# An attention and expert-routing kernel: one exponential a unit, the diagonal of the maxima on GpSimd, and transposes moved behind the scores

## The reference

```
x = layernorm(x + attention(x, x, x, causal))                  # self
x = layernorm(x + attention(x, encoder_output, encoder_output)) # cross
x = layernorm(x + moe(x))                                      # 8 experts, 2 a token, FF = 512
attention: scores = q k / sqrt(8); a = softmax(scores); o = a v; o @ wo + bo
```

## Time and profile before

| what | value |
|---|---|
| time, median of 3 runs | 798.61 us (795.01 to 799.62) |
| the profiled execution | 803.89 us |
| its span | 802.1 us |
| TensorE busy (matmuls) | 596.7 us, 74% |
| weight loads | 471.7 us, 59% |
| VectorE | 488.9 us, 61% |
| ScalarE | 453.3 us, 57% |
| GpSimd | 370.1 us, 46% |
| mean granted clock of TensorE | 0.876 of full speed |

### The profile page before, as it was taken

How to read it: one execution, slowest core, us unless ns; L and a number is a source line. 1 busy time by engine, 2 the same in 40 slices (tenths; PEclk the granted TensorE clock), 3 DMA queues, 4 the chain that set the end, 5 groups by cost and what they waited for, 6 DMA issues and landing times. The chain is left out here.

```text
span 802.1 us, 21265 instructions
## 1 busy us (share of the span) xinstructions
PE 596.7 (74%) x7870; PEld 471.7 (59%) x7870; DVE 488.9 (61%) x1337; ACT 453.3 (57%) x824; POOL 370.1 (46%) x576
## 2 busy tenths in 40 slices
PE   2776676776767698887987988698777776878970
PEld 1344444545444476765766776476666666777870
DVE  3465879767696877888776578866334651221153
ACT  1223545444333589977997889688467554334320
POOL 7122243433337544435753665387237476530350
PEclk9965878877757999998999999899989888899995
DMA  4351554843132645544655675546546457778730
GB/s 111 106 174 54 161 170 128 287 125 87 34 93 66 198 146 168 164 130 139 195 155 177 185 205 171 151 140 174 162 142 191 141 176 222 234 239 266 234 96 20
DMA packets 141413, 124.64 MB, mean 155 GB/s; under 512 B 12224, under 2 KB 123600, under 8 KB 141312
## 3 DMA queue, kind: packets, MB, share of 16 engines
q1 hardware_dynamic: 134496, 113.06, 46.6%
q0 software_dynamic: 4368, 9.05, 4.1%
q10 hardware_dynamic: 2448, 1.18, 0.5%
HBM read 86.81 MB, written 38.54 MB: 156 GB/s over the span
## 5 line engine op out<-in xcount | busy, mean ns | idle before, releaser
L1089 DVE TENSOR_REDUCE row_max<-bank 128x16 bf16<-128x1024 f32 x64 | 78.3, 1224 | 79.4 <-PE bank L1501 78.6
L776 POOL TENSOR_TENSOR prob_lo<-probT,prob_hi 128x384 f16<-128x384 f32 x64 | 68.7, 1073 | 92.8 <-ACT prob_hi L892 92.4
L1549 PE MATMUL bank<-consts,o_n 128*128 128x64 f32 x256 | 47.7, 316 | 81.2 <-DVE o_n L1108 71.6
L1628 PE MATMUL bank<-w_in,w_hl 128*128 128x128 f32 x704 | 106.3, 298 | 0.0
L1549 PEld LDWEIGHTS bank<-consts,o_n 128*128 128x128 f32 x256 | 39.3, 220 | 95.3 <-issue 71.0
L1628 PEld LDWEIGHTS bank<-w_in,w_hl 128*128 128x128 f32 x704 | 93.8, 207 | 0.4
L889 ACT ACTIVATE probT<-bank 128x1024 f32<-128x1024 f32 x64 | 65.6, 1024 | 46.2 <-PE bank L1525 45.8
L762 POOL TENSOR_TENSOR veps<-mv,eps 128x1 f32<-128x1 f32 x64 | 14.5, 226 | 140.3 <-DVE mv L1127 140.3
L799 POOL DMA_INDIRECT w_hl<-ys,pos x60 | 59.6, 994 | 40.5 <-DMA ys<-w_hl 23.5
L1614 PE MATMUL bank<-xT,w_in 128*128 128x128 f16 x1056 | 77.9, 226 | 0.0
L1082 DVE TENSOR_TENSOR prob_lo<-probT,prob_hi 128x640 f16<-128x640 f32 x64 | 62.3, 973 | 24.9 <-ACT prob_hi L892 24.8
(11 more groups left out here) (173 smaller groups left out, 1556.8 us busy)
## 6 DMA issues: line engine op xcount, KB each, us to landing
w_in<-w_scr SPq DMA_DIRECT2D x96, 512.0 KB, 3.7
q_scr<-q_hl SPq DMA_DIRECT2D x64, 128.0 KB
k_scr<-k_hl SPq DMA_DIRECT2D x64, 128.0 KB, 2.3
q_st<-q_scr SPq DMA_DIRECT2D x32, 256.0 KB, 3.9
k_all<-k_scr SPq DMA_DIRECT2D x128, 64.0 KB, 2.1
xs_tile<-xs SPq DMA_DIRECT2D x42, 128.0 KB
ys<-w_hl SPq DMA_DIRECT2D x42, 128.0 KB, 2.1
xs<-xs_tile SPq DMA_DIRECT2D x3, 1472.0 KB, 6.8
```

The costliest lines, as they stand in the source:

```text
L776: pool.tensor_tensor(p_lo[u.buf][:, h, :], probT[u.buf][:, h, :], p_hi[u.buf][:, h, :], ALU.subtract).then_inc(lo_second[u.kind], 1)
L1089: dve.reduce_max(row_max[u.buf][:, :], bank[:, SC:SC + 2, :].rearrange("p a (h k) -> p (a h) k", k=S), AX.X).then_inc(max_done[a], 1)
L1549: last = pe.matmul(turned_o[:, 64 * b:64 * b + 64], o_n[u.buf][:, b, :, :, :].rearrange("p c a d -> p (c a d)"), consts[:, C_DELTA:C_TRI], ...
L1628: last = pe.matmul(expert_y(x), hid[x.par][:, c, :], w2_t[x.wb][:, c, :], start=False, stop=c == FC - 1, skip_group_check=True)
```

## The change

1. `exps` keeps only the float32 exponential. VectorE makes `p_hi` by a copy of `probT` to float16 (1024 elements a partition), waits for its own semaphore, and subtracts all 1024 elements for `p_lo`. GpSimd's share of `p_lo` is gone.
2. The product that makes `max_diag` moves from VectorE to GpSimd (`spread_maxima`), behind `gain` and before the scatters. It waits for `max_done`, across engines now.
3. In slots with no tile that close no chunk, before the end of attention (slots -5 to 32), TensorE does `turn_o` and `turn_y` behind `scores_T` and `scores`, and ScalarE copies them out behind `exps`. Other slots keep them at the head.

`weigh` waits for `lo_done` in place of two semaphores. No transfer is added or moved.

```diff
@@ -23,7 +23,6 @@
 W1_SCALE = 64.0
 W1_SLOT = 8
 CLEAR_SLOT, CLEAR_EVERY = 10, 2
-DVE_HEADS = 10
 
 
 
@@ -224,6 +223,11 @@
 
 def tiles_in(slot):
     return [Tile(m) for m in range(NMOE) if TILE_SLOT[m] == slot]
+
+
+def turns_late(slot):
+
+    return not tiles_in(slot) and chunk_closes(slot) is None and slot < ATTENTION_END
 
 
 def chunk_opens(slot):
@@ -489,7 +493,7 @@
         b12_hi_ready, b12_lo_ready = sem("b12_hi_ready"), sem("b12_lo_ready")
         x2_hi_ready, x2_lo_ready = sem("x2_hi_ready"), sem("x2_lo_ready")
         v_hi_ready = two("v_hi_ready")
-        lo_first, lo_second = two("probs_lo_first_heads"), two("probs_lo_second_heads")
+        hi_done, lo_done = two("probs_hi"), two("probs_lo")
         lg_ready, lg_done, route = sem("lg_ready"), sem("lg_done"), sem("route_step")
 
         less_ready, exp_of_less = sem("logits_and_second_less_first"), sem("their_exps")
@@ -769,12 +773,12 @@
                 n = u.tile()
                 pool.tensor_tensor(x2_hl[:, n, D:2 * D], x_rows[:, n, :], x2_hl[:, n, 0:D], ALU.subtract).then_inc(x2_lo_ready, 1)
 
-            def probs_low(u):
-
-                pool.wait_ge(exp_done[u.kind], u.count())
-                h = slice(DVE_HEADS, H)
-                pool.tensor_tensor(p_lo[u.buf][:, h, :], probT[u.buf][:, h, :], p_hi[u.buf][:, h, :], ALU.subtract).then_inc(
-                    lo_second[u.kind], 1)
+            def spread_maxima(u):
+
+                pool.wait_ge(max_done[u.kind], u.count())
+                m = row_max[u.buf][:, :].rearrange("p (a c) -> p a c", c=2).unsqueeze(2).to_broadcast([P, HP, S, 2])
+                dl = neg_delta.rearrange("p (q c) -> p q c", c=2).unsqueeze(1).to_broadcast([P, HP, S, 2])
+                pool.tensor_tensor(max_diag[u.buf][:, :, :, :], dl, m, ALU.mult).then_inc(diag_ready[u.kind], 1)
 
             def scatter(c, t, k):
 
@@ -826,6 +830,8 @@
                     add_bo(Block(t + 1))
                 if u := unit_at(g - 4):
                     gain(u)
+                if u := unit_at(g):
+                    spread_maxima(u)
                 for c, n, k in scatters_at(g):
                     scatter(c, n, k)
                 if (f := group_in(g, ROOT)) is not None and at_end(f):
@@ -834,8 +840,6 @@
                     fetch_picks(f)
                 if (f := group_in(g, ROOT)) is not None and not at_end(f):
                     last_spread(f)
-                if u := unit_at(g - 1):
-                    probs_low(u)
                 if u := unit_at(g - 3):
                     spread(u)
                 if (u := unit_at(g - 6)) and u.kind == CROSS:
@@ -887,9 +891,6 @@
                 if v:
                     act.wait_ge(pv_ready[v.kind], v.count())
                 act.activation(probT[u.buf][:, :, :].rearrange("p h q -> p (h q)"),
-                               bank[:, KEYS:KEYS + 2, :].rearrange("p a n -> p (a n)"), ACT.Exp,
-                               scale=float(HD) ** -0.5)
-                act.activation(p_hi[u.buf][:, :, :].rearrange("p h q -> p (h q)"),
                                bank[:, KEYS:KEYS + 2, :].rearrange("p a n -> p (a n)"), ACT.Exp,
                                scale=float(HD) ** -0.5).then_inc(exp_done[a], 1)
 
@@ -914,6 +915,14 @@
                     act.wait_ge(lg_ready, Unit(CROSS, b.back(1), u.pair).count())
                 act.activation(x2_tile[u.buf][:, :], turned_y, ACT.Identity,
                                bias=ln_bc[a][:, :], scale=ln_gc[a][:, :]).then_inc(yT_done[a], 1)
+
+            def both_turned(g):
+                if u := unit_at(g - 5):
+                    act.wait_ge(yT_ready[u.kind], u.count())
+                if u := unit_at(g - 3):
+                    o_turned(u, same_buffers(g - 3))
+                if u := unit_at(g - 5):
+                    y_turned(u)
 
             def x2_high(u):
 
@@ -982,16 +991,14 @@
                     act.wait_ge(w_in, 16 * WEIGHTS)
                 if g == 4:
                     act.wait_ge(late_in, 16 * LATE_WEIGHTS)
-                if u := unit_at(g - 5):
-                    act.wait_ge(yT_ready[u.kind], u.count())
-                if u := unit_at(g - 3):
-                    o_turned(u, same_buffers(g - 3))
-                if u := unit_at(g - 5):
-                    y_turned(u)
+                if not turns_late(g):
+                    both_turned(g)
                 if (c := chunk_closes(g)) is not None:
                     copy_y(Tile(FIRST_TILE[c] + TILES_OF[c] - 1))
                 if u := unit_at(g - 1):
                     exps(u, same_buffers(g - 1))
+                if turns_late(g):
+                    both_turned(g)
                 for x in tiles[:1]:
                     tile_step(x)
                 if s == 0 and ca.exists():
@@ -1075,12 +1082,15 @@
                                              ALU.subtract)
                 last.then_inc(v_done[a], 1)
 
-            def probs_low(u):
+            def probs_low(u, v):
 
                 dve.wait_ge(exp_done[u.kind], u.count())
-                h = slice(0, DVE_HEADS)
-                dve.tensor_tensor(p_lo[u.buf][:, h, :], probT[u.buf][:, h, :], p_hi[u.buf][:, h, :], ALU.subtract).then_inc(
-                    lo_first[u.kind], 1)
+                if v:
+                    dve.wait_ge(pv_ready[v.kind], v.count())
+                dve.tensor_copy(p_hi[u.buf][:, :, :], probT[u.buf][:, :, :]).then_inc(hi_done[u.kind], 1)
+                dve.wait_ge(hi_done[u.kind], u.count())
+                dve.tensor_tensor(p_lo[u.buf][:, :, :], probT[u.buf][:, :, :], p_hi[u.buf][:, :, :], ALU.subtract).then_inc(
+                    lo_done[u.kind], 1)
 
             def maxima(u):
 
@@ -1088,10 +1098,6 @@
                 dve.wait_ge(s_ready[a], u.count())
                 dve.reduce_max(row_max[u.buf][:, :],
                                bank[:, SC:SC + 2, :].rearrange("p a (h k) -> p (a h) k", k=S), AX.X).then_inc(max_done[a], 1)
-                dve.wait_ge(max_done[a], u.count())
-                m = row_max[u.buf][:, :].rearrange("p (a c) -> p a c", c=2).unsqueeze(2).to_broadcast([P, HP, S, 2])
-                dl = neg_delta.rearrange("p (q c) -> p q c", c=2).unsqueeze(1).to_broadcast([P, HP, S, 2])
-                dve.tensor_tensor(max_diag[u.buf][:, :, :, :], dl, m, ALU.mult).then_inc(diag_ready[a], 1)
 
             def outputs(u):
 
@@ -1357,7 +1363,7 @@
                 if u := unit_at(g):
                     maxima(u)
                 if u := unit_at(g - 1):
-                    probs_low(u)
+                    probs_low(u, same_buffers(g - 1))
 
                 if u := unit_at(g - 2):
                     dve.wait_ge(pv_ready[u.kind], u.count())
@@ -1530,8 +1536,7 @@
             def weigh(u):
 
                 a, b = u.kind, u.blk
-                pe.wait_ge(lo_first[a], u.count())
-                pe.wait_ge(lo_second[a], u.count())
+                pe.wait_ge(lo_done[a], u.count())
                 pe.wait_ge(v_done[a], b.times(1, 1))
                 for p in range(HP):
                     ph, pl = [v[u.buf][:, 2 * p:2 * p + 2, :].rearrange("p h q -> p (h q)") for v in (p_hi, p_lo)]
@@ -1561,6 +1566,15 @@
                 pe.wait_ge(yn_ready[u.kind], u.count())
                 pe.transpose(turned_y, yn[u.buf][:, :], ident).then_inc(yT_ready[u.kind], 1)
                 turned.append((yT_done[u.kind], u.count()))
+
+            def turn_both(g):
+                u, v = unit_at(g - 3), unit_at(g - 5)
+                if u or v:
+                    turn_free()
+                if u:
+                    turn_o(u)
+                if v:
+                    turn_y(v)
 
             def logits(u):
                 pe.wait_ge(yT_done[CROSS], u.count())
@@ -1680,19 +1694,16 @@
                     pe.wait_ge(zeroed, ZEROED)
                 if g == 4:
                     pe.wait_ge(late_in, 16 * LATE_WEIGHTS)
-                u, v = unit_at(g - 3), unit_at(g - 5)
-                if u or v:
-                    turn_free()
-                if u:
-                    turn_o(u)
-                if v:
-                    turn_y(v)
+                if not turns_late(g):
+                    turn_both(g)
                 if (c := chunk_closes(g)) is not None:
                     down(Tile(FIRST_TILE[c] + TILES_OF[c] - 1))
                 if u := unit_at(g - 1):
                     scores_T(g, u)
                 if u := unit_at(g):
                     scores(g, u)
+                if turns_late(g):
+                    turn_both(g)
                 for x in tiles[:1]:
                     if y := x.near(1):
                         turn_tile(y)
```

## The result

The changed kernel is slower: a median of 872.2 us (867.8 to 874.2) against 799.0 us, ratio 1.092, 95% interval 1.086 to 1.098. Its profiled execution took 871.0 us, its span is 869.2 us.

A forecast was written before the change was run, and what follows sets the result against it. No engine was full; a loop through o_n, maxima and scores set the pace. Terms +3 + 6 + 29 + 16 - 7 = +47 on the 803.9 us profile gave 851, so a median of 845 us, range 803 to 893.

The forecast's parts named there:

- stage A: Slots 8 to 32, no expert tiles: late transposes cut the o_n loop, but VectorE's load grows to 206.5 against 201, +6 us.
- The port: VectorE and GpSimd take turns by whole instructions; waiting GpSimd goes first, so VectorE's p_lo stands while the diagonal runs.
- the first rival: GpSimd's diagonal does not stand in VectorE's way; slots 8 to 32 gain 16 us, 779 us in all, chance 0.12.
- The diagonal, d: Length of the diagonal product on GpSimd: 2.18 us for 1024 elements, replacing 0.69 us on VectorE.
- Stage B: 19 units, mostly one tile a slot: o_n late by 1.93 us a slot, 0.23 of it slack; 17 x 1.70 = +29 us.
- the other loop: Slots 8 to 32: maxima 1.3, copy and diagonal 2.7, both scores 3.8; 7.8 us a slot, hidden under VectorE's 8.3.
- GpSimd's queue: Diagonal stands before the scatters, rstd and norm; counted as nothing, though a norm 0.5 late would lose 7 us.
- Stage C: Slots 50 to 63, every other with two tiles: seven lose 14.7 us, three 1.3 together, four nothing; +16 us.
- the single exponential, -7: Removes 1.02 us of ScalarE a unit; nothing in slots 8 to 49, 6.7 us in the last-ending chain between 444 and 621.
- The first slots: Latency chain from 27 to 75 us: diagonal +1.5, one exponential -1.0, copy and longer p_lo +1.0; +3 over two blocks.
- The cheap and the dear diagonal: Rivals on the GpSimd product's length: 1.17 us gives 793 us, chance 0.07; 3.4 us gives 910 us, chance 0.06.
- the two waits for o_n: Sign of being right: TensorE's wait for o_n gone from slots 8 to 32 and grown in the one-tile slots after.

The follow-up runs named there:

- spare product: Changed kernel with the diagonal back on VectorE, plus a same-size GpSimd product into a spare tensor nobody reads, started by the maxima: 902.5 us.
- TensorE kept busy: Changed kernel plus eight throwaway matmuls at the head of one-tile slots from 33 to 63: 864.4 us, ratio 1.086.
- outputs first, diagonal on GpSimd: Changed kernel with VectorE's cast and p_lo moved behind outputs and residual from slot 33 on: 813.9 us, ratio 1.022.
- outputs first, diagonal on VectorE: Changed kernel with the diagonal back on VectorE, and cast and p_lo behind outputs and residual from slot 33 on: 770.2 us, ratio 0.966.
- late transposes and outputs first, two exponentials: Kernel before plus late transposes, and VectorE's share of p_lo behind outputs and residual from slot 33 on; p_lo stays split: 778.5 us, ratio 0.977.
- fully ordered kernels: Late transposes, diagonal on VectorE, VectorE's p_lo (and any cast) behind outputs and residual in every slot: 767.9 us with one exponential, 773.4 with two.

## Why the prediction came out as it did

Direction and mechanism were right, and so was the costliest stretch: 872 us lies in the range of 803 to 893, 27 us above the 845. Of these 27, 20 are in the stages, where the sum said +47 and the profiles say +67, most of it in stage A. The other 7 come almost wholly from the step from profile to median: the profiled execution of before was 5.3 us above its median, which I took off, and that of the changed kernel is 1.2 us below its own.

**A slip in the prediction's count.** The window of 75 to 276 us holds 24 starts of the maxima, not the 25 units of slots 8 to 32. These take 208.2 us, 8.33 a slot in place of 8.04. With the prediction's own terms for 25 units, VectorE's load is 210.7 us, and stage A comes out at +2 instead of +6, further from the measured +16.9.

**The port, as forecast.** "GpSimd, once waiting, goes ahead of the next VectorE instruction" held in 54 of 64 units, and where p_lo had started first the diagonal stood instead. Shown three ways: by the p_lo of 2.80 us against 1.22, by a spare product that costs 107 us though nobody waits for it, and by an order that lets the same product run under port-free work and gives 58 us back. The sign that was to decide for the first rival, p_lo starting under 0.1 us after the copy, was badly chosen: p_lo is issued 0.04 us after the copy (372.61 after 372.57) and then stands. Its duration and its end tell, not its start.

**The diagonal, d.** 2.18 forecast from the rows and an estimated 2.2 beside it; 1.90 alone and 2.27 with its wait, so both were too high. With 1.90 in place of 2.18, o_n was done 4.54 us after the maxima in slots 33 to 49, not 4.85.

**Stage B, +29 forecast, +31.4 measured: right for partly the wrong reason.** With 4.54 the term is 17 x (4.54 - 2.92 - 0.23) = 24. That the sum came within 2.4 us is luck: a diagonal taken too dear stood in for some 7 us that I had left out. The run with TensorE kept busy puts 5.4 of these down to the clock. The later o_n leaves TensorE idle, its clock drops, and the scores that follow in the same loop run at the lower level. In these kernels:

| kernel | o_n after the maxima (us) | TensorE's clock | slots 33 to 50 (us) |
|---|---|---|---|
| outputs first, diagonal on GpSimd | 1.39 | 0.96 | 136.8 |
| outputs first, diagonal on VectorE | 1.94 | 0.96 | 134.6 |
| late transposes and outputs first, two exponentials | 2.03 | 0.97 | 134.9 |
| before | 2.92 | 0.96 | 138.9 |
| diagonal on VectorE | 3.71 | 0.95 | 146.4 |
| changed | 4.54 | 0.87 | 170.3 |
| spare product | 5.36 | 0.81 | 193.4 |

Below 2.9 us this distance does not order the kernels: 1.39 is no faster than 1.94. From 2.92 to 3.71 the 0.79 us costs (146.4 - 138.9) / 17 = 0.4 a slot. From 3.71 to 5.36 each 0.83 us costs (170.3 - 146.4) / 17 = 1.4 us a slot, 0.6 more than itself, and the granted clock falls with it. Filling the idle time gave 5.4 us of it back in this stretch; whether all of the 0.6 is the clock is not shown.

**Stage A, +6 forecast, +16.9 measured: the mis-sized term.** VectorE's load came out as worked out (192.5 us busy, 199.4 forecast), but it stood idle for 32.6 us, not 7.1. The step that failed is "the other loop ... is 7.8 a slot and hidden under VectorE's 8.3". It was not hidden in every slot: in some the other loop ended last, in others VectorE did. Read slot by slot from the timelines of slots 8 to 30, the maxima take 1.2 us, the diagonal is ready 2.4 us after them, and from then to the end of the scores it takes 3.4 us on average (3.8 forecast). The two blocks of scores alone take 1.7 to 4.9 us in all slots but one, of 7.7. In slot 24 the two blocks take 4.84 us, behind an idle time of 2.66 and at a granted clock of 0.50:

```profile
218.50 1.03 PE L1519 MATMUL bank<-max_diag,consts_bf 128*128 128x512 bf16 x2 [2.66 <-POOL max_diag L781]
...
222.28 1.06 PE L1507 MATMUL bank<-k_all,q_st 128*64 128x256 f16 x8
```

In slot 25, at 1.00, they take 2.12. In 6 of the 23 slots the next maxima follow within 0.1 us of the scores, so TensorE came last. In 16 they follow 0.5 us later or more, because VectorE had not come to them yet; the mean of all 23 is 1.9. So the loop was on average no longer than forecast (7.0 us), and what failed is that it was hidden. Each slot takes the longer of the two, and the sum of the longer ones (9.0 us a slot) is more than the longer of the two averages (8.3). This is read from the trace; no run takes the variation away. TensorE waited 46.0 us for the diagonal in these slots. Getting the cast and p_lo out of the diagonal's way, the amount of work unchanged, took 19 us off. A term that I put at nothing, GpSimd's queue, is not cleared: VectorE's wait for rstd grew from 7.7 to 13.4 us in this stage and from 32.4 to 53.7 over the whole kernel, and no run took it alone. What the fully ordered kernels still wait for in these slots (198 us with one exponential, 192 with two) stays open; the trace has waits for the diagonal, for the transfers of q and k and for projections, and no run here took one of them alone.

**Stage C, +16 forecast, +17.1 measured, and the single exponential, -7.** No gain is shown in the changed kernel. The -3.9 us after slot 63 lies within what the same instructions spread there (253.1 us in the kernel before, 247.2 with late transposes alone), and from slot 63 to the maxima of slot 71 the changed kernel lost 4.4 (65.8 against 61.4). In the old order, with the diagonal on VectorE, the single exponential with its cast and p_lo cost 16 us. Once o_n was out of the way, it took 4.1 us off slots 50 to 63 and some 3 to 7 off slots 63 to 71. With outputs first in every slot, it took 5.8 (122.0 against 127.8) and 2.8 (56.8 against 59.6). So the gain exists, but not in the order of work that the prediction was about. The first slots cost 5.6 us instead of 3; with the diagonal on VectorE they reach slot 8 at 72.4 us and not at 81.1, so that too was the GpSimd diagonal.

**The rivals.** The faster one (no standing at the port) was ruled out by p_lo's duration. Its mechanism, the loop through o_n cut by late transposes, was right for the part that it concerned: the late transposes alone took 15.1 us off slots 8 to 33, where that rival said 16 (23, with 8.33 us a slot). That the whole came to 779.9 us and the rival said 779 is a coincidence, since it was worked out for one exponential and another diagonal. The cheap and the dear diagonal are out by 1.90.

**The signs.** The durations of the diagonal (2.27) and of p_lo (2.80) and the two waits for o_n came as listed, and slots 34 to 40 took 8.2 to 10.8 us, 9.5 on average. One sign failed, with stage A: VectorE was busy for 133.4 of 160.7 us in slots 16 to 32, 83% and not over 95, and in five of these 17 slots it stood idle before the maxima.

## What to carry to other kernels

Before moving an elementwise operation from VectorE to GpSimd, ask what VectorE does in the same stretch: a subtraction of two SBUF tensors or a float32 cast there stood for the whole GpSimd instruction (1.22 us became 2.80, 0.68 became 2.38). If PSUM-fed work can go in its place, most of the loss goes: here the same instructions in another order were 78 us faster. The move still did not pay, since the same order with the product on VectorE was 26 us faster again. Split a change of several parts into its parts first: the transposes alone were worth 19 us, and the change as a whole, 73 us slower, hid that under a loss of 92. When two loops take turns at being last, add up the longer one slot by slot; the longer of the two averages is too short. Where a late operand leaves TensorE idle, look at the granted clock: here it fell from 0.96 to 0.87 over a stretch, and part of the loss was its.

## What the runs showed that I had not expected

A spare product of 2.4 us a unit, waited for by nobody, costs 107 us in 796, 1.7 us a unit. A GpSimd instruction of one element a partition took 1.54 us instead of 0.55 behind a VectorE subtraction, so the port stops small work as well as large. Less a start of 0.17 us, as in the rows of the other GpSimd products, the diagonal on GpSimd cost 1.7 ns an element, against 1.96 in those rows. They differ in types, operation and layout, so what saves the 0.3 is not shown.
